# A decoder layer on one core: the position bias goes through 14 skewed copies in DRAM in place of 112, and the first loads get semaphores of their own

## What is computed

```python
scores = jnp.einsum('bhsd,bhkd->bhsk', q, k)          # 16 heads, 112 queries, 375 keys
rel = jnp.arange(K)[None, :] - jnp.arange(S)[:, None]
buckets = _relative_position_bucket(rel)              # 32 buckets
bias = rel_bias[buckets].transpose(2, 0, 1)[None]     # the same for all 32 sequences
scores = scores + bias
attn = jax.nn.softmax(scores.astype(jnp.float32), axis=-1)
```

## Time and profile before

| | |
|---|---|
| median of 3 runs | 1335.68 us (1335.61 to 1335.86) |
| the profiled execution, its own time | 1333.42 us |
| its span (first to last instruction) | 1331.8 us |
| PE busy | 1227.9 us, 92% of the span |
| DVE, ACT, POOL busy | 870.9, 728.9, 859.0 us |
| mean granted clock of PE | 0.967 of full speed |

### The profile page before, as it was taken

The page is one execution under the profiler, slowest core; times in us unless marked ns, Lnnn a source line. Parts: engine busy times, 40 slices in busy tenths (PEclk is TensorE's granted clock), DMA queues, the critical chain, the costliest instruction groups (busy, mean ns, idle before and its releaser), DMA issues. The chain is left out here.

```text
span 1331.8 us, 40106 instructions
## 1 busy us (share of the span) xinstructions
PE 1227.9 (92%) x13828; PEld 1090.0 (82%) x13829; DVE 870.9 (65%) x3949; ACT 728.9 (55%) x1827; POOL 859.0 (65%) x1597
## 2 busy tenths in 40 slices
PE   5399999999999999999999999995399999999993
PEld 3388888888888888888888888884399999999993
DVE  2266888788878887887778877786244444444441
ACT  2256666666666666666666666663244444444440
POOL 4267787887878787878787878765244444444431
PEclk8889999999999999999999999997699999999997
DMA  8910100111011101110011001101476222222224
GB/s 164 158 62 24 43 27 28 35 45 29 27 35 35 40 27 31 35 43 28 27 38 43 28 28 31 28 13 40 157 201 152 50 49 48 48 48 47 46 39 126
DMA packets 47316, 73.20 MB, mean 55 GB/s; under 512 B 6832, under 2 KB 34032, under 8 KB 47088
## 3 DMA queue, kind: packets, MB, share of 16 engines
q1 hardware_dynamic: 31408, 45.74, 13.0%
q0 software_dynamic: 15744, 25.31, 9.8%
HBM read 46.90 MB, written 27.80 MB: 56 GB/s over the span
## 5 line engine op out<-in xcount | busy, mean ns | idle before, releaser
L470 POOL TENSOR_SCALAR arena<-arena,mC 112x375 f32<-112x375 f32 x512 | 299.5, 598 | 136.9 <-DVE mC L857 136.7
L857 DVE CUSTOM_DVE_ANT_0 arena<-bank_S,arena 112x375 f32<-112x375 f32 x512 | 264.9, 543 | 112.6 <-PE bank_S L599 64.8
L1099 POOL DMA_INDIRECT acc<-y,xb x64 | 119.4, 1866 | 206.5 <-DVE y L1243 182.9
L476 POOL TENSOR_SCALAR arena<-arena,mF 112x112 f32<-112x112 f32 x512 | 177.6, 367 | 22.8 <-DVE mF L845 21.2
L741 ACT ACTIVATE pTC<-bank_Q 126x336 f32<-126x336 f32 x286 | 128.6, 450 | 45.7 <-PE bank_Q L609 44.5
L707 ACT ACTIVATE arena<-bank_B 128x224 f32<-128x224 f32 (+5 forms) x229 | 87.4, 382 | 110.0 <-PE bank_B L530 35.0
L707 ACT ACTIVATE arena<-bank_A 128x224 f32<-128x224 f32 (+3 forms) x219 | 82.2, 376 | 112.0 <-PE bank_A L622 28.1
L1230 DVE SCALAR_TENSOR_TENSOR hT<-bankU,gub,gate 128x128 f32<-128x128 f32 x256 | 72.1, 344 | 107.4 <-PE bankU L1139 95.1
L609 PE MATMUL bank_Q<-ident,arena 112*126 112x112 f32 x858 | 130.8, 261 | 0.5 <-ACT pTC L741 0.5
L1139 PE MATMUL bankG<-xbT,gwb 128*128 128x128 f32 x1024 | 126.6, 277 | 1.0 <-ACT gwb L1186 1.0
L1139 PE MATMUL bankU<-xbT,uwb 128*128 128x128 f32 x1024 | 124.8, 275 | 0.0
(11 more groups left out here) (206 smaller groups left out, 2926.8 us busy)
## 6 DMA issues: line engine op xcount, KB each, us to landing
arena<-in_l_ctxT SPq DMA_DIRECT2D x32, 378.0 KB, 3.6
xb<-xs POOLq DMA_DIRECT2D x64, 129.0 KB, 3.5
arena<-in_L_ffn_gate_w SPq DMA_DIRECT2D x8, 512.0 KB, 4.4
arena<-in_L_ffn_up_w SPq DMA_DIRECT2D x8, 512.0 KB, 5.4
arena<-in_L_ffn_down_w SPq DMA_DIRECT2D x8, 512.0 KB, 3.7
arena<-in_x SPq DMA_DIRECT2D x32, 112.0 KB, 2.1
acc<-arena SPq DMA_DIRECT2D x32, 112.0 KB, 1.9
out<-acc SPq DMA_DIRECT2D x4, 896.0 KB, 9.1
```

The lines of the kernel that those rows point to most:

```text
L470: pool.tensor_scalar(z[n % NZ][:, 0:T], z[n % NZ][:, 0:T], -1.0, mC[:, n:n + 1], ALU.mult, ALU.add).then_inc(s_u, 1)
L476: m = pool.tensor_scalar(sF[r][:, j, :], sF[r][:, j, :], -1.0, mF[:, r, j:j + 1], ALU.mult, ALU.add)
L857: dve.tensor_tensor_reduce(out=z[n % NZ][:, 0:T], in0=bank[f"S{r}"][0:S, 0:T], in1=nbias[:, n, :], scale=1.0, scalar=3.0e38, op0=ALU.add, ...
L1099: pool.indirect_dma_start(out=acc[:, :], out_offset=bass.IndirectOffsetOnAxis(ap=xb[x][:, D + 1:D + 2].bitcast(I32), axis=0), in_=y2[x % 2 ...
```

## The change

Five things are done together.

- `skew` has 14 copies (`SK`) in place of 112. It is written by two DMAs of 16 x 14 x 243 in place of 16 x 112 x 243, and read back by eight DMAs of 14 partitions each, every one from the same 14 copies with a start that is 14 elements lower than that of the part before.
- The order of SP's queue is another: the writes of `skew` come right after the weights `wkv`, ahead of the row load of sequence 2 and of the eight late constants; the reads of `nbias` come behind those constants, and the row load of sequence 3 and the context load of sequence 1 come behind the reads.
- The one-hot matrix, the bucket table, `rowid` and `iota` are issued by ACT in place of SP.
- `s_const` is split: each engine waits for the load that it uses, at the first place that uses it. `wkv` counts on a semaphore of its own and no longer on `s_late`.
- POOL makes only `power` at the start; its other fills (`fill_constants`) come after `rs1` of sequence 0. ACT does one Exp of one column ahead of `xn` of sequence 0.

```diff
+    SK = 14
+    assert S % SK == 0
...
-    skew = nc.dram_tensor("skew", (S, H, S + T - 1), F32, kind="Internal").ap()
+    skew = nc.dram_tensor("skew", (SK, H, U), F32, kind="Internal").ap()
...
                     load_x(0)
-                    for n, (dst, src) in enumerate(consts):
-                        sp.dma_start(dst, src).then_inc(s_const if n < NCONST else s_late, 16)
-                        if n == NCONST - 1:
-                            load_x(1)
-                            load_c(0)
-                    for b in range(2, NX):
+                    sp.dma_start(ident[:, :], a["c_ident"]).then_inc(s_ident, 16)
+                    sp.dma_start(wqk[:, :, :], a["l_wqk"].rearrange("(c p) n -> p c n", p=P)).then_inc(s_wqk, 16)
+                    sp.dma_start(hmask[:, :], a["c_half_mask"]).then_inc(s_mask, 16)
+                    sp.dma_start(wv[:, :, :], a["l_wv"].rearrange("(c p) n -> p c n", p=P)).then_inc(s_wv, 16)
+                    sp.dma_start(window[:, :], a["c_window"]).then_inc(s_mask, 16)
+                    load_x(1)
+                    load_c(0)
+                    sp.dma_start(wkv_in[:, :, :], a["l_wkv"].rearrange("(c p) n -> p c n", p=P)).then_inc(s_wkv0, 16)
+
+                    sp.wait_ge(s_fc, 1)
+                    for i, (o, w) in enumerate(((0, U // 2), (U // 2, U - U // 2))):
+                        sp.dma_start(skew.rearrange("s h u -> h s u")[:, :, o:o + w],
+                                     fbias[i].rearrange("h (o u) -> h o u", o=1).to_broadcast([H, SK, w])).then_inc(s_skw, 16)
+                    load_x(2)
+                    for dst, src in late:
+                        sp.dma_start(dst, src).then_inc(s_late, 16)
+                    sp.wait_ge(s_skw, 32)
+                    for s0 in range(0, S, SK):
+                        skewed = bass.AP(skew.tensor, S - 1 - s0, [[H * U - 1, SK], [U, H], [1, T]])
+                        sp.dma_start(nbias[s0:s0 + SK, :, :], skewed).then_inc(s_nb, 16)
+                    for b in range(3, NX):
                         load_x(b)
                     load_c(1)
-
-                    need(sp, s_fc, 1)
-                    for i, (o, w) in enumerate(((0, U // 2), (U // 2, U - U // 2))):
-                        sp.dma_start(skew.rearrange("s h u -> h s u")[:, :, o:o + w],
-                                     fbias[i].rearrange("h (o u) -> h o u", o=1).to_broadcast([H, S, w])).then_inc(s_skw, 16)
-                    need(sp, s_skw, 32)
-                    skewed = bass.AP(skew.tensor, S - 1, [[H * U - 1, S], [U, H], [1, T]])
-                    sp.dma_start(nbias[:, :, :], skewed).then_inc(s_nb, 16)
...
-                    pool.memset(power[:, :], -0.5)
...
+                    pool.memset(power[:, :], -0.5).then_inc(s_power, 1)
+                    pool.wait_ge(s_power, 1)
...
                             deviation(int(step[2]) - 1, b)
+                            if step == "rs1" and b == 0:
+                                fill_constants()
...
-                    need(pe, s_const, 16 * NCONST)
+                    pe.wait_ge(s_rows0, 16 * 3)
...
                 def _(act):
+                    act.dma_start(one_hot[:, 0:U // 2], a["c_one_hot"][:, 0:U // 2]).then_inc(s_rows0, 16)
+                    act.dma_start(one_hot2[:, 0:U - U // 2], a["c_one_hot"][:, U // 2:U]).then_inc(s_rows0, 16)
+                    act.dma_start(relb[:, :], a["L0_xattn_rel_bias"]).then_inc(s_rows0, 16)
+                    act.dma_start(rowid[:, :], a["c_row"]).then_inc(s_const, 16)
+                    act.dma_start(iota[:, :], a["c_iota"]).then_inc(s_const, 16)
+                    act.wait_ge(s_power, 1)
+                    act.activation(nmx[:, :], power[:, :], ACT.Exp)
...
                         if b == 0:
-                            need(dve, s_nb, 16)
+                            dve.wait_ge(s_nb, 16 * (S // SK))
```

More of the change, by code:

```diff
@@ L288, in decoder_layer @@
             drained = {n: sem(f"drained_{n}") for n in "ABPQS"}
+            s_power = sem("power_ready")
+            s_ident = sem("identity_loaded")
+            s_wqk = sem("query_key_weights_loaded")
+            s_wv = sem("value_weights_loaded")
+            s_mask = sem("masks_loaded")
+            s_rows0 = sem("bias_table_loaded")
             s_late = sem("late_constants_loaded")
+            s_wkv0 = sem("context_weights_loaded")
             s_pool = sem("pool_constants_ready")
@@ L366, in _ @@
                 def _(sp):
[L367 to L376, removed]
+                    late = [
                         (wout[:, :, :], a["L0_attn_W_out"].rearrange("(c p) n -> p c n", p=P)),
@@ L384, in _ @@
                     ]
-                    assert len(consts) == NCONST + NLATE
+                    assert len(late) == NLATE
                     def load_x(b):
@@ L439, in link, with fill_constants @@
                         pool.wait_ge(s_plc, linked[0])
-                    pool.memset(power[:, :], -0.5)
[L442 to L450, removed]
+                    pool.memset(power[:, :], -0.5).then_inc(s_power, 1)
+                    pool.wait_ge(s_power, 1)
+                    def fill_constants():
+                        link(pool.memset(vS[:, :, :], 0.0))
+                        pool.memset(vS[:, :, DH:DH + 1], 1.0).then_inc(s_pool, 1)
+                        for q in range(2):
+                            link(pool.memset(v2[q][:, :, :, :], 0.0))
+                            pool.memset(v2[q][:, :, :, DH:DH + 1], 1.0)
+                        for i in range(NZ):
+                            pool.memset(z[i][:, T:TPAD], MASKED)
+                        pool.memset(ones[:, :], 1.0).then_inc(s_pool, 1)
                     def deviation(i, b):
@@ L462, in mask_keys @@
                         drained_wait(pool, "qk", b)
+                        if b == 0:
+                            pool.wait_ge(s_mask, 32)
                         for p in range(2):
@@ L497, in _ @@
                             scatter(b)
[L499 removed]
+                    pool.wait_ge(s_padi, 1)
                     for e in range(E):
@@ L554, in self_values @@
                         drained_wait(pe, "v", b)
+                        if b == 0:
+                            pe.wait_ge(s_pool, 1)
                         for r in range(HG):
@@ L636, in _ @@
                             continue
-                        if not late and step in ("wo", "k0", "k1", "v0", "v1", "q2"):
+                        if not late and step in ("wo", "q2"):
                             late = True
-                            need(pe, s_late, 16 * NLATE)
+                            pe.wait_ge(s_late, 16 * NLATE)
                         if b == 0 and step in ("k0", "k1", "v0", "v1"):
-                            need(pe, s_wkv, 1)
+                            pe.wait_ge(s_wkv, 1)
                         B_, F_ = fill_wait(pe, step, b), fill_sem(step, b)
                         if place[step, b] in (("A", 0), ("B", 0)):
-                            need(pe, s_fc, 1)
+                            pe.wait_ge(s_fc, 1)
                         if step == "xT":
+                            if b == 0:
+                                pe.wait_ge(s_ident, 16)
                             need(pe, s_xn, b + 1)
@@ L648, in _ @@
                         elif step == "qk":
+                            if b == 0:
+                                pe.wait_ge(s_wqk, 16)
                             queries_keys(b, B_, F_)
                         elif step == "v":
+                            if b == 0:
+                                pe.wait_ge(s_wv, 16)
                             drained_wait(pe, "xT", b)
@@ L721, in halves @@
                         B_ = filled_wait(act, "q2", b)
-                        if b >= 2:
+                        if b == 0:
+                            act.wait_ge(s_mask, 32)
+                        elif b >= 2:
                             filled_wait(act, "S3", b - 2)
@@ L840, in masked @@
                         filled_wait(dve, "S4", b)
-                        if b:
+                        if b == 0:
+                            dve.wait_ge(s_mask, 32)
+                        else:
                             filled_wait(dve, f"sT{r}", b - 1)
```

29 lines of the change are left out of this document (14 added, 15 removed).

## The result

The changed kernel takes 1315.8 us in the median of four runs (1313.9 to 1317.1), against 1335.8 us before: 20.0 us less, a ratio of 0.9845 with a 95% interval of 0.9829 to 0.986. The forecast was 1312.0, its range 1307.5 to 1319.5. The profiled execution took 1313.9 us, so against that of before 19.5 us are to be explained.

The account below looks back on a forecast made before the run. The prediction took the start of the pipeline, with its stall of about 18.0 us for `nbias`, as the bound: 21.7 us by the first `t` plus 2.0 for the clock, 23.7 less, gives 1312.0 us, range 1307.5 to 1319.5.

Parts of the forecast that it names:

- What bounds the kernel: Before the first `t`: scores stand ready about 18.0 us while only the bias is missing, a stall wholly on the path.
- Part 1, the start: Start of the pipeline: `xT` of sequence 0 at 7.4 in place of 11.67, taken as 4.0 us earlier; scores at 43.6.
- Part 2, the bias: Writes and reads of the bias: `skew` written at 14.1, reads from 17.2 take 25 us, to 42.2.
- the slow end: Reads of `nbias`: 28.3 us if the eight parts run one behind the other at 95 GB/s, against 13.6 side by side.
- The rule on ports: Reads of `nbias`: bandwidth follows how many of 16 ports the partitions reach, four neighbours sharing one; 24.7 us or more.
- What is late next: Ahead of the first `t`: DVE waits from 40.8 to 43.2 for the rows of sequence 3; `t0` at 43.9.
- Part 3, the clock: PE's work behind the old stall: without long idle time the clock stays high, 2.0 us less, bounds 0 and 3.
- The sum: Whole kernel: 21.7 us by the first `t` plus 2.0 for the clock, 23.7 us less, 1312.0 us.
- The late bias: Reads of the bias take 32 us, `t0` at 51.1, 16.5 us less, 1319.2 us; chance 0.17.
- The start does not move: Another load holds up `xT` or `qk`; scores at 47.6 as before, bias hidden, 1315.7 us; chance 0.10.
- Nothing moves: The steady stretch takes up the gain by a lower clock or worse interleaving; about 1335 us; chance 0.02.
- slower: Eight narrow reads take over 48 us, so `nbias` lands later than before; 1349 us at 45 GB/s; chance 0.03.

Follow-up runs that it names:

- copies_only: The kernel before with 14 copies of `skew` and eight reads, its start and queue order kept: 1315.4 us, ratio 0.9859.
- start_only: The changed kernel with 112 copies of `skew` and one read of 112 partitions again: 1336.3 us, ratio 1.0017.

## Why the prediction was right, and where it was off

**What bounds the kernel.** Right. The stall for `nbias` was on the path whole, and its end is the gain: 18.25 of 19.5 us are there by the first `t`, and `copies_only`, which removes nothing else, has the whole gain.

**Part 1, the start.** Right as far as it went: `xT` at 7.80 against 7.4, 3.9 us earlier against 4.0, with `s_fc` deciding. The bucket table landed half a microsecond later than I took (5.20). POOL's fills ended at 9.58, and the second `deviation` at 10.62 waited for DVE's statistics, not for them: they cost nothing. The step that failed is the next one, "With 4.0 the scores `S0` are ready at 43.6": they were ready at 47.2. The self scores still came 3.4 us earlier (34.43 for 37.82), the eight projections 3.2 (38.90 for 42.08), and then it was lost, because PE's clock was at its lower level. The eight and sixteen projections took 2.05 and 3.62 us, and 1.15 and 1.95 before. I had priced the half clock behind the old stall and not asked whether pauses of PE in the prologue bring it elsewhere. The run with PE kept busy and narrow reads shows that it needs the pauses: the changed kernel with them filled has the clock at 1.00 from 20 to 44 us and its scores 5.1 us earlier. A pause does not bring it each time. The kernel before has a first stretch too (0.57 and 0.58 in the windows 26 to 30 and 30 to 34 us) and no second one at 38 to 46 us, nor have `copies_only` and the spread reads with the rows first; what decides it is open.

**Part 2, the bias.** The choice of the slow end was right, its size was not. The eight reads were issued at 16.58, not at 14.4: SP did not wait for the writes at all, it was held in issuing. The rows of sequence 2 and the late constants took it from 8.64 to 16.54, 7.9 us where I had counted them at 0.46 each. Since the loads ahead of them set their start, that cost little: their first piece ran at 17.6, the forecast had 17.2. From 17.2 on I gave the reads 25 us and the rows of sequence 3 one more, 43.2. These landed at 46.7 (issued at 20.43, 26.3 us to landing). This term of the sum was too small by 3 us: the pieces of the bias ran for 28.0 us, nearly the 28.3 of the slow end. The reason given, narrow parts, is shown by the spread reads, 16.6 us against 28.0. The rule on ports therefore told more than its agreement with the 95 GB/s: it was the reason to believe the slow row and not the fast one. That 28.0 is so near 28.3 is luck in part. Reads from 16 neighbours ran at 111 GB/s and not at the 95 of the writes from 16 partitions, and parts of 14 then cost about an eighth again; the two nearly cancel.

**What is late next.** Right in kind: DVE waited for the rows of sequence 3 ahead of `t0`, 4.14 us in place of 2.4. That the scores would be there too, within half a microsecond, was the forecast as well; both were some 3.5 us later than I had them, for two different reasons. With either one alone off, the first `t` would have been nearly as late.

**Part 3, the clock.** I took 2.0 us. The clock's own price is what comes back between the first and the last `t`: 2.9 us, near the upper bound of 3. Nine other profiles give 2.2 to 3.0 in the same way. In the passage to the experts, which the prediction did not look at, this pair of executions gives 1.8 back, so that 1.2 are left; that this belongs to the change is not shown.

**The sum.** 21.7 + 2.0 = 23.7 were forecast; the profiles give 18.25 + 1.2 = 19.5, the medians 20.0. Of the 4.2 us between them 3.4 are the first `t`, 47.34 in place of 43.9, and 0.8 what follows it. That the forecast of 1312.0 and the measured 1315.8 are so close rests on the old stall, which was read rightly; the two paths to the new first `t` were both misread by about the same amount.

**The rivals.** The late bias was half true: its read time was 28.0 us and not 32, and the first `t` at 47 us and not 51. "The start does not move" gave 1315.7 us, the measured number, by the wrong road: the start did move and was taken back later. Nothing moves, and slower, found no support here; `start_only` has shown what would have made it slower, the order of the queue with large writes in it, and this I had not seen. I had costed the move of the rows of sequence 2 behind the writes at nothing without naming its condition.

## What to carry to other kernels

When a load is cut into parts, look at which partitions each part touches and not only at its bytes: eight parts of 14 neighbours took 28.0 us, the same parts with a stride of 8 partitions 16.6, and seven parts of 16 neighbours 24.2. When a long wait is removed, write down the time of everything that ends shortly before it, since two limits at the same place hide each other: alone, the faster reads moved the first step from 47.34 to 46.31 us and the busy PE to 48.44; both, with the rows first, moved it to 41.70. Do not take such places from one trace: the landing of one load moved by 1.7 us and a stretch of half clock came or stayed away between executions. Ask of every pause of PE in a prologue what it does to the clock of the work behind it, and of every load that is moved in a queue how long what now stands ahead of it will be.

## What was not expected of the hardware

Fifty-one useless matmuls made the kernel faster by 0.26% (0.9802 against 0.9828, intervals that just overlap, with the first `t` 3.15 us earlier), by holding the clock at 1.00 where it fell to 0.50 after pauses of 0.7 to 2.4 us. With them the runs of one kernel also agreed better (1306.4 to 1307.9 against 1308.2 to 1313.1; the other two kernels with them differ by 0.9 and 1.5 us from run to run, the changed kernels without by 1.9 to 5, the kernel before by 1.5 to 2.6). And a queue that issues a DMA in 0.46 us needed 1.99 and 2.39 us for two right behind the writes of `skew`, so that issuing nine loads took 7.9 us; behind the reads of the bias one took 6.29 us. That the queue waits there for the transfers ahead of it is the likely reading, and was not tested.
